# A two-layer decoder in one kernel: squares of three layer norms on ScalarE, the low part of the cached keys on VectorE, the query split shared between two engines

## The reference, cut to what matters

```
x = x + L0_attn(layernorm(x))             # autocorrelation: FFT, top-k lags, weighted shifts
x = x + L0_xattn(layernorm(x), ctx, ...)  # fake-quantised product with the context
x = x + L0_ffn(layernorm(x), ...)         # MX block-quantised gated feed-forward
x = x + L1_attn(layernorm(x), ...)        # 32 heads, 8 kv heads, rotary, cached and new keys
x = x + L1_xattn(layernorm(x), ctx, ...)  # 16 heads, 4 kv heads
x = x + L1_ffn(layernorm(x), ...)         # top-2 of 8 experts

layernorm(x) = (x - mean(x)) / sqrt(var(x) + 1e-5)      # over the 512 columns
```

## Time and profile before

| | us |
|---|---|
| median of 3 runs | 1362.09 (1361.77 to 1364.2) |
| the profiled execution | 1362.19 |
| its span (first to last instruction) | 1360.4 |

### The profile page before, as it was taken

One profiled execution on the slowest core, in us unless ns is written; L12 is line 12 of the kernel. 1 busy time (PEld: TensorE's weight loads), 2 busy tenths in 40 slices (PEclk: granted clock), 3 DMA queues, 4 the chain that ended last, 5 costly groups with the idle time before them and its releaser, 6 DMA issues.

```text
span 1360.4 us, 16919 instructions
## 1 busy us (share of the span) xinstructions
PE 1159.0 (85%) x5660; PEld 879.0 (65%) x5660; DVE 942.6 (69%) x1483; ACT 528.1 (39%) x1042; POOL 556.8 (41%) x382
## 2 busy tenths in 40 slices
PE   4939622668799999999999999879799999987999
PEld 2413311227487878787878787755587888875887
DVE  7998999976577777777777777645355555543543
ACT  1211210222465555555555555532353444342111
POOL 3774531310255555555555554420454544441000
PEclk9968955788999999999999999988999999999899
DMA  7172442001100101010101000151001000001122
GB/s 285 63 232 89 151 170 70 24 0 48 57 24 20 55 20 54 19 54 19 54 19 53 20 31 12 55 163 24 6 13 28 20 9 20 1 24 62 35 99 84
DMA packets 38834, 77.70 MB, mean 57 GB/s; under 512 B 11395, under 2 KB 19588, under 8 KB 35588
## 3 DMA queue, kind: packets, MB, share of 16 engines
q1 hardware_dynamic: 37188, 71.86, 16.1%
q0 software_dynamic: 1600, 5.24, 1.2%
HBM read 69.75 MB, written 9.44 MB: 58 GB/s over the span
## 4 chain that ended last, share of the span: by engine, by line
PE 66%; DVE 23%; issue 7%; ACT 3%; POOL 1%; DMA 0%; DVEq 0%; POOLq 0%; ACTq 0%
PE PS L1427 14%; PE PS L1425 14%; PE PS L1426 14%; PE PS L1491 9%; PE PS L1465 5%; DVE nmax L1103 3%; PE PS L1342 2%; DVE PTL L1144 2%; DVE blkamax L909 1%; PE PS L1596 1%; DVE QTH L1096 1%; PE PS L1290 1%; PE PS L1274 1%; DVE QTL L1098 1%; PE PS L1393 1%
## 5 line engine op out<-in xcount | busy, mean ns | idle before, releaser
L561 POOL TENSOR_TENSOR arena<-arena,rsum 128x768 f32<-128x768 f32 x192 | 285.3, 1486 | 466.7 <-DVE rsum L1108 466.7
L1103 DVE TENSOR_REDUCE nmax<-PS 128x1 f32<-128x768 f32 x192 | 183.3, 955 | 195.3 <-PE PS L1427 194.0
L729 ACT ACTIVATE arena<-PS,nmax 128x768 f32<-128x768 f32 x192 | 173.4, 903 | 270.1 <-DVE nmax L1103 270.0
L1491 PE MATMUL PS<-identf,arena 128*128 128x128 f32 x1152 | 160.2, 275 | 32.5 <-DVE PTL L1144 19.8
L1491 PEld LDWEIGHTS PS<-identf,arena 128*128 128x128 f32 x1152 | 133.8, 140 | 70.3 <-issue 46.4
L1144 DVE TENSOR_TENSOR PTL<-PS,PTH 128x384 fp32r<-128x384 f32 x256 | 129.7, 548 | 1.8 <-ACT PTH L745 1.1
L745 ACT ACTIVATE PTH<-PS 128x384 fp32r<-128x384 f32 x256 | 111.6, 488 | 37.7 <-PE PS L1491 34.5
L1465 PE MATMUL PS<-arena 128*96 128x256 f32 x384 | 87.5, 379 | 0.0
L1098 DVE TENSOR_TENSOR QTL<-arena,QTH 128x512 fp32r<-128x512 f32 (+1 forms) x48 | 79.3, 1653 | 1.7
L1425 PE MATMUL PS<-WOH,OTH 128*128 128x512 f32 (+1 forms) x192 | 76.6, 399 | 4.1 <-DVE OTL L1121 3.0
L544 POOL TENSOR_TENSOR WQL<-arena,WQH 128x512 fp32r<-128x512 f32 (+1 forms) x48 | 57.7, 1205 | 49.9 <-ACT WQH L614 49.9
(11 more groups left out here) (242 smaller groups left out, 2543.6 us busy)
## 6 DMA issues: line engine op xcount, KB each, us to landing
arena<-in_wq SPq DMA_DIRECT2D x32, 256.0 KB, 2.6
arena<-in_wo SPq DMA_DIRECT2D x8, 1024.0 KB, 4.9
arena<-in_expert_w SPq DMA_DIRECT2D x8, 1024.0 KB, 4.8
arena<-in_wgu SPq DMA_DIRECT2D x11, 512.0 KB, 3.9
arena<-v_dram SPq DMA_DIRECT2D x8, 384.0 KB, 3.4
arena<-in_wq SPq DMA_DIRECT2D x16, 192.0 KB, 2.9
arena<-in_wo SPq DMA_DIRECT2D x4, 768.0 KB, 5.6
arena<-in_wd SPq DMA_DIRECT2D x4, 704.0 KB, 4.0
```

What stands on the lines that cost most here:

```text
L561: pool.tensor_tensor(PR[:, u % 4, :], PR[:, u % 4, :], rsum[:, u % 4:u % 4 + 1].broadcast_to([P, KEYS]), ALU.mult).then_inc(s["pn_ready"], 1)
L729: act.activation(PR[:, slot, :], SC[pair][:, 0:KEYS], ACT.Exp, bias=nmax[:, slot:slot + 1], accum_out=psum_exp[:, slot:slot + 1]).then_inc ...
L1103: dve.tensor_reduce(nmax[:, slot:slot + 1], SC[pair][:, 0:KEYS], AX.X, ALU.max, negate=True)\
L1491: mm = pe.transpose(bank(B_PT[half])[:, k * P:(k + 1) * P], PR[:, u % 4, c * P:(c + 1) * P], identf[:])
```

## The change

1. Norms 0 to 2: VectorE no longer centres and squares. It writes `neg_mean`, the negative of the mean, and ScalarE makes `H = (X - mean)^2` in one instruction for each row tile, with the function Square and the bias `neg_mean` (new function `squared`). GpSimd keeps only the power. `squared(0)` stands first on ScalarE, `squared(1)` behind its last weight step, `squared(2)` behind `quantised_out` of the context product.
2. `KCL` leaves GpSimd's list, where it stood between norm 2 and the query weights, and goes to VectorE, behind the third of four `down_added`.
3. The query split: ScalarE writes `QTH` (`queries_hi`) behind the exponential of the unit in which VectorE used to split; VectorE keeps only the subtraction (`queries_lo`), which stands ahead of the row maximum of the next unit.

```
 def layer_norm(stage):                      # GpSimd
-    if stage < 3:
-        for r in range(2, RT):
-            pool.wait_ge(s["ln_centred"], RT * stage + 2 * r - 3)
-            pool.tensor_tensor(H[:, r, :], H[:, r, :], H[:, r, :], ALU.mult).then_inc(s["ln_squared_p"], 1)
     pool.wait_ge(s["ln_var"], stage + 1)
...
-            for b in range(0, NSEL, 4):     # GpSimd, behind layer_norm(2)
-                pool.wait_ge(s["kch_ready"], b // 4 + 1)
-                pool.tensor_tensor(fr(KCL[:, b:b + 4]), KC[:, b:b + 4], KCH[:, b:b + 4], ALU.subtract)\
-                    .then_inc(s["kcl_ready"], 1)
...
+            def squared(stage):             # ScalarE
+                act.wait_ge(s["ln_mean"], stage + 1)
+                for r in range(RT):
+                    act.activation(H[:, r, :], X[:, r, :], ACT.Square, bias=neg_mean[:, r:r + 1])\
+                       .then_inc(s["ln_squared"], 1)
...
+                def queries_hi(G, j):       # ScalarE
+                    act.wait_ge(s["q_raw"], KPAIRS + GH * G + j + 1)
+                    act.activation(fr(QTH[0:hd, j, :]), QT[0:hd, j, :], ACT.Copy).then_inc(s["q_hi"], 1)
...
                             exps(U + 2, (u + 2) % 4, u % 2)
+                        if tail and u == 2:
+                            queries_hi(g, GH - 1)
+                        if u in Q_HI and not last:
+                            queries_hi(g + 1, Q_HI[u])
...
                     summed(mean_var[:, :, 0])   # VectorE
+                    dve.tensor_scalar(neg_mean[:], mean_var[:, :, 0], -1.0 / D, None, ALU.mult)\
+                       .then_inc(s["ln_mean"], 1)
                     step(dve.tensor_scalar(mean_var[:, :, 0], mean_var[:, :, 0], 1.0 / D, None, ALU.mult))
-                    for r in (2, 0, 3, 1):
-                        dve.tensor_scalar(H[:, r, :], X[:, r, :], mean_var[:, r, 0:1], None, ALU.subtract)\
-                           .then_inc(s["ln_centred"], 1)
-                    for r in range(2):
-                        dve.wait_ge(s["ln_centred"], RT * stage + 2 * (r + 1))
-                        dve.tensor_tensor(H[:, r, :], H[:, r, :], H[:, r, :], ALU.mult).then_inc(s["ln_squared_d"], 1)
                     for r in range(RT):
...
+                        dve.wait_ge(s["ln_squared"], RT * stage + r + 1)
                         ins = dve.tensor_reduce(parts[:, r, :], H[:, r, :].rearrange("p (b e) -> p b e", e=8),
                                                 AX.X, ALU.add)
...
+            for b in range(0, NSEL, 4):     # VectorE, ahead of the last down_added
+                dve.wait_ge(s["kch_ready"], b // 4 + 1)
+                dve.tensor_tensor(fr(KCL[:, b:b + 4]), KC[:, b:b + 4], KCH[:, b:b + 4], ALU.subtract)\
+                    .then_inc(s["kcl_ready"], 1)
             down_added(RT - 1)
...
+                def queries_lo(G, j):       # VectorE
+                    dve.wait_ge(s["q_hi"], KPAIRS + GH * G + j + 1)
+                    dve.tensor_tensor(fr(QTL[0:hd, j, :]), QT[0:hd, j, :], QTH[0:hd, j, :], ALU.subtract)\
+                       .then_inc(s["q_ready"], 1)
```

More of the change, by code:

```diff
@@ L50 @@
 Q_OUT = {6: 0, 9: 1, 12: 2}
-Q_SPLIT = {7: 0, 10: 1, 13: 2}
+Q_HI = {7: 0, 10: 1, 13: 2}
+Q_SPLIT = {8: 0, 11: 1, 14: 2}
 V_OUT = {8: 0, 11: 1, 14: 2}
@@ L78, in decoder_kernel @@
         mean_var = sb("mean_var", [P, RT, 2])
+        neg_mean = sb("neg_mean", [P, RT])
         parts2 = sb("parts2", [P, RT, D // 64])
@@ L255, in decoder_kernel @@
             consts ident rowbase_done iota_done pool_chain dve_chain
-            ln_stats ln_centred ln_squared_d ln_squared_p ln_var ln_rstd h_ready ht_psum ht_act ht_dve
+            ln_stats ln_mean ln_squared ln_var ln_rstd h_ready ht_psum ht_act ht_dve
             dft_psum sq_ready power_ready corr_psum tap_diff tap_exp off_ready tapw_ready dg_ready tap_psum tap_added
@@ L650, in tap_diagonals @@
                        .then_inc(s["dg_ready"], 1)
+            squared(0)
             transposed(0)
@@ L664, in _ @@
                     context_step(n)
+            squared(1)
             def quantised_out(r, bk, psum, ready):
@@ L672, in _ @@
                 quantised_out(r, r, "at_psum", "at_ready")
+            squared(2)
             quantised_out(0, 6, "hqt_psum", "hqt_ready")
@@ L864, in layer_norm @@
                     summed(mean_var[:, :, 0])
+                    dve.tensor_scalar(neg_mean[:], mean_var[:, :, 0], -1.0 / D, None, ALU.mult)\
+                       .then_inc(s["ln_mean"], 1)
                     step(dve.tensor_scalar(mean_var[:, :, 0], mean_var[:, :, 0], 1.0 / D, None, ALU.mult))
-                    for r in (2, 0, 3, 1):
-                        dve.tensor_scalar(H[:, r, :], X[:, r, :], mean_var[:, r, 0:1], None, ALU.subtract)\
-                           .then_inc(s["ln_centred"], 1)
-                    for r in range(2):
-                        dve.wait_ge(s["ln_centred"], RT * stage + 2 * (r + 1))
-                        dve.tensor_tensor(H[:, r, :], H[:, r, :], H[:, r, :], ALU.mult).then_inc(s["ln_squared_d"], 1)
                     for r in range(RT):
-                        if r < 2:
-                            dve.wait_ge(s["ln_squared_d"], 2 * stage + r + 1)
-                        else:
-                            dve.wait_ge(s["ln_squared_p"], 2 * stage + r - 1)
+                        dve.wait_ge(s["ln_squared"], RT * stage + r + 1)
                         ins = dve.tensor_reduce(parts[:, r, :], H[:, r, :].rearrange("p (b e) -> p b e", e=8),
@@ L1113, in queries_out @@
                         rotate(n, B_MISC, QT[:, j, :], rope_q)
-                def queries_split(G, j):
-                    split_rows(KPAIRS + GH * G + j, QTL[0:hd, j, :], QT[0:hd, j, :], QTH[0:hd, j, :])
+                def queries_lo(G, j):
+                    dve.wait_ge(s["q_hi"], KPAIRS + GH * G + j + 1)
+                    dve.tensor_tensor(fr(QTL[0:hd, j, :]), QT[0:hd, j, :], QTH[0:hd, j, :], ALU.subtract)\
+                       .then_inc(s["q_ready"], 1)
                 def head_out(G, j):
@@ L1135, in group @@
                             head_out(g - 1, GH - 1)
+                        if tail and u == 3:
+                            queries_lo(g, GH - 1)
+                        if u in Q_SPLIT and not last:
+                            queries_lo(g + 1, Q_SPLIT[u])
                         scored = not (last and u >= UNITS - 2)
@@ L1162, in group @@
                             output_added(g - 1, u - 2, Y_BANKS[u - 2])
-                        if tail and u == 2:
-                            queries_split(g, GH - 1)
-                        if u in Q_SPLIT and not last:
-                            queries_split(g + 1, Q_SPLIT[u])
                 row_max(UNITS * first, 0, 0)
```

## The result

| | before | changed |
|---|---|---|
| median, us | 1362.07 (4 runs) | 1347.48 (4 runs) |
| lowest to highest | 1361.77 to 1364.2 | 1342.07 to 1350.41 |
| profiled execution, us | 1362.19 | 1347.69 |
| its span | 1360.4 | 1345.8 |

The ratio is 0.9894, with a 95% interval of 0.9868 to 0.992. The kernel is faster, by 14.6 us and not by the 20.5 forecast, and 1347.5 lies 1.5 us above the range. One of its four executions, 1342.07, lay within it. These four lie 8.3 us apart, against 2.4 for the kernel before; but beside the later runs the kernel before had executions from 1355.5 to 1365.9 us, so it is no steadier.

A forecast was written before the change was run, and what follows sets the result against it. TensorE was taken to bound the first attention, VectorE the norms and the feed-forward after norm 2. Terms 2.4 + 3.55 + 3.55 + 7.1 - 0.3 + 3.5 + 0.7 = 20.5 us gave a median of 1341.6, range 1338.0 to 1346.0.

The forecast's parts named there:

- norms 1 and 2: Between mean and last sum of squares, Squares on ScalarE leave VectorE limiting: 3.55 us saved in each norm.
- norm 0: VectorE is 3.55 us earlier but waits for the `cs` load until 21.2; weight chunks start 2.4 us earlier (1.4 to 3.55).
- `KCL` off GpSimd: Feed-forward after norm 2: VectorE's tiles 1 to 3 no longer stand still, `gate_up(1)` starts earlier, 7.1 us saved.
- On VectorE `KCL`: Last down product: four subtractions plus GpSimd's `WQL` slightly overfill a 5.80 us gap, 0.3 us lost (0 to 0.5).
- the query split: First attention: less TensorE waiting, 3.5 us from the split of unit 2 and 0.7 from that of unit 13.
- the wait in unit 3: First attention: TensorE's wait for `PTL`, 0.47 or 0.55 us in seven groups, goes: 3.5 us.
- unit 14: First attention, behind unit 13's split: TensorE's wait of 0.74 us shrinks to about 0.64, seven times, 0.7 us gained.
- that nothing in the second attention changes: Second attention: the only waits are 0.22 to 0.25 us, of the scores-to-transposes loop, so the split gains nothing.
- another clock in attention than 1.00: Sign against the forecast: TensorE's granted clock in attention differing from 1.00.
- Clock rivals: Feed-forward clock: higher, with norm 0 giving more, 1338.5 us, chance 0.13; or lower, up to 1345.5, chance 0.10.
- the clock gives less: Rival, feed-forward: later products run at 1.2 GHz, 1344.4 us at worst, 1345.5 with norm 0 low; chance 0.10.

The follow-up runs named there:

- neg_last_2: Changed kernel with the tile `neg_mean` allocated behind the arena, no instruction different, second run: 1335.62 us, ratio 0.9818 to the kernel before.
- no_kcl: Changed kernel with `KCL`'s four subtractions back on GpSimd behind norm 2, none on VectorE: 1354.84 us, ratio 0.9941 to the kernel before.
- again_2: Changed kernel as it stands, a later run on the same chip as `neg_last_2`: 1350.11 us, ratio 0.9904 to the kernel before.
- f_first: Changed kernel plus six unread TensorE products in each of units 2, 3, 4 of the second attention's first group: 1341.38 us, ratio 0.9859.

## Why the prediction was wrong, point by point

**Right: norms 1 and 2.** From mean to last sum 3.49 us instead of 7.08, 3.6 each (3.55 forecast), VectorE limiting as assumed.

**Partly: norm 0.** The wait for `cs` came, but the gain was 1.2 and not 2.4: the load landed at 21.57 instead of 21.2, and L991 then took 1.01 us instead of 0.17, beside GpSimd's work that starts at 21.95. This is just under the low end that was named (1.4), with the collision as its reason. In `neg_last_2` the load lands at 21.1 and the gain is 2.25, so the size was partly a matter of when the load landed in this execution.

**Right: `KCL` off GpSimd.** `gate_up(1)` came 6.75 us earlier beyond the norms (7.1 forecast); `no_kcl` gives 7.15 back. On VectorE `KCL` cost nothing, not 0.3, though GpSimd's `WQL` was stretched to 2.01 us.

**Right in kind, too small: the query split.** 4.2 forecast, 5.8 measured. The mis-sized term is the price of the wait in unit 3. The rows showed 0.47 or 0.55, but the unit that it delays took 5.19 us where its neighbours took 4.47, and the next one 4.60: 0.72 + 0.13, and 0.1 for unit 14. A wait's bracket holds only what stands ahead of that row; the spacing of the units holds all.

**The step that failed: that nothing in the second attention changes.** The prediction took "nothing" there, since "the only waits are 0.22 to 0.25". That reading is wrong: the trace of before has waits of 1.61 us too, in the short units (975.70 and 979.20 above), and these are the units that grew. The prediction listed "another clock in attention than 1.00" as what would prove it wrong. It did: 4.83 us in the first group and 2.0 in the last of the profiled execution, 3.2 and 5.15 in `again_2` (0.15 and 0.4 of these are the address's, below). Clock rivals were drawn for the feed-forward alone, where the clock was seen to change; the units where TensorE was 5.18 of 10 us busy at a clock of 1.00 stood in the trace and were not asked what they would cost at 1.2 GHz.

**The second one: a declaration.** `neg_mean = sb(...)` is no instruction, and the prediction has no term for it. It cost 3.6 us in TensorE's products, hidden in part behind the split's larger gain (six groups gave 3.34 net, near the forecast, as 5.25 less 1.9), and in this kernel most of the clock's loss went with it: with the tile behind the arena the same instructions take 1335.6 to 1338.1 us. That is 25.4 and 26.9 us under the kernel before on the same chips, more than the 20.5 forecast, so the terms of the sum are not confirmed as a whole by that either; between the profiled executions it is 21.3 and 26.3.

The balance against the forecast of 20.5: 1.4 less before the attention, 1.1 more in the first attention with its tail (the split's excess and a slow spot of the kernel before, less the address), 0.65 more at norm 4, 4.83 + 0.72 + 1.99 less in the second attention, 1.26 more behind it: 5.9 us, the miss.

The rival "the clock gives less" (1344.4 to 1345.5) named the clock, but in the feed-forward, where it did not come, and it was 2 us too small. Nor did the range allow for how far the executions of one kernel lie apart, 8 us here: the miss of the median by 1.5 us is smaller than that, while the 5.9 us against the forecast are found stretch by stretch in the profiled execution.

## What to carry to other kernels

List the stretches where the bound engine is half idle and still at its upper clock, and price them at the lower one, even if the change doesn't touch them: here they were worth 0 to 8 us in the profiled executions. Put a new small tile behind the large ones, or ahead of all of them, not between, or compare the spacing of equal instructions before crediting or blaming an edit. Price a stall by the spacing of the units around it, not by its bracket.

## What the runs showed of the hardware that was not expected

- The spacing of TensorE's 512-column products of 32-bit data depends on where the tiles lie relative to each other: an output unit takes 4.44 us, 4.51 with one region moved by 32 bytes, 4.44 again with all moved by 32.
- The granted clock falls to 1.2 GHz in units that TensorE fills by about half, in some executions and not in others of the same kernel. A unit then takes 5.04 us instead of 3.50, and with unread products in its idle time it takes 3.50 again (`f_first`).
- That fall goes with the arena's place: in the last group it came in 7 of 9 profiles with the arena alone 32 bytes on, in 0 of 8 otherwise. The cause is not shown.
